# Multi-head attention stage of a four-stage graph kernel: input side one chunk ahead, statistics two ahead, capped rows in two buffers

## The reference

```python
def graph_attention(x, bias, W, a_src, a_dst):
    h = jnp.einsum('bnd,dhk->bhnk', x, W.reshape(D, H, Dh))
    s = jnp.einsum('bhnk,hk->bhn', h, a_src)
    t = jnp.einsum('bhnk,hk->bhn', h, a_dst)
    e = jax.nn.leaky_relu(s[:, :, :, None] + t[:, :, None, :], ALPHA)
    e = e + bias[:, None, :, :]
    attn = jax.nn.softmax(e, axis=-1)
    out = jnp.einsum('bhij,bhjk->bhik', attn, h)
    return out.transpose(0, 2, 1, 3).reshape(B, N, H * Dh)
attn_in = layer_norm(x, g1, b1)
attn = graph_attention(attn_in, bias, W1, a_src1, a_dst1) + x
attn_in2 = layer_norm(attn, g2, b2)
out = graph_attention(attn_in2, bias, W2, a_src2, a_dst2) + attn
```

## Time and profile before

| what | value |
| --- | --- |
| median of 3 runs | 1226.5 us (1225.91 to 1226.75) |
| profiled execution | 1226.1 us, its span 1224.3 us |
| TensorE, VectorE, ScalarE, GpSimd busy | 92%, 64%, 61%, 35% of the span |
| multi-head stage | about 798 to 1078 us of the span |
| single-head stage | about 1078 to the end |

### The profile page before, as it was taken

One profiled execution on the slowest core, in us unless ns is written; L12 is line 12 of the kernel. 1 busy time (PEld: TensorE's weight loads), 2 busy tenths in 40 slices (PEclk: granted clock), 3 DMA queues, 4 the chain that ended last, 5 costly groups with the idle time before them and its releaser, 6 DMA issues.

```text
span 1224.3 us, 41293 instructions
## 1 busy us (share of the span) xinstructions
PE 1127.3 (92%) x16156; PEld 984.7 (80%) x16156; DVE 781.3 (64%) x1908; ACT 743.7 (61%) x1766; POOL 426.7 (35%) x641
## 2 busy tenths in 40 slices
PE   5799999999999899999999999978888888869998
PEld 5588888888888788998998998966667777658886
DVE  6676777777677745545445445456556665558886
ACT  2577767777776645445445446465656656548986
POOL 2532111211121012312212213225566555567664
PEclk9799999999999999999999999998778877779999
DMA  8020100110000000000000000000000000002112
GB/s 224 1 71 29 54 28 28 28 53 28 28 20 12 2 1 1 1 1 0 0 0 0 0 0 0 1 20 21 17 17 9 17 17 10 3 2 70 62 57 86
DMA packets 41736, 31.18 MB, mean 25 GB/s; under 512 B 5280, under 2 KB 41376, under 8 KB 41632
## 3 DMA queue, kind: packets, MB, share of 16 engines
q1 hardware_dynamic: 36736, 28.84, 7.5%
q10 hardware_dynamic: 4896, 0.80, 0.6%
HBM read 21.25 MB, written 8.39 MB: 24 GB/s over the span
## 4 chain that ended last, share of the span: by engine, by line
PE 71%; ACT 9%; DVE 8%; issue 6%; POOL 3%; ACTq 1%; DVEq 1%; DMA 0%; POOLq 0%
PE BK L1320 5%; PE BK L1198 5%; PE BK L1197 5%; PE BK L1196 5%; PE BK L1404 5%; PE BK L1405 5%; PE BK L1406 5%; PE BK L1294 4%; PE F L1196 4%; PE BK L1306 4%; PE F L1221 3%; PE F L1197 3%; PE F L1198 3%; PE BK L1287 3%; ACT xn L1005 2%
## 5 line engine op out<-in xcount | busy, mean ns | idle before, releaser
L862 POOL TENSOR_TENSOR ve<-mv,eps_l 128x4 f32<-128x4 f32 x64 | 15.1, 236 | 533.0 <-DVE mv L300 533.0
L1066 ACT ACTIVATE gf<-BK,bcol 128x512 f32<-128x512 f32 x128 | 88.1, 688 | 178.6 <-PE BK L1198 167.8
L985 ACT ACTIVATE e_sb<-BK,nmx 128x128 f32<-128x128 f32 x512 | 141.4, 402 | 28.5 <-DVE nmx L460 28.5
L1404 PE MATMUL BK<-wf_hi,gh 128*128 128x256 f32 x512 | 142.9, 279 | 0.0
L1405 PE MATMUL BK<-wf_hi,gl 128*128 128x256 f32 x512 | 141.6, 277 | 0.0
L1406 PE MATMUL BK<-wf_lo,gh 128*128 128x256 f32 x512 | 141.5, 276 | 0.0
L553 DVE TENSOR_TENSOR gl<-gf,gh 128x512 fp32r<-128x512 f32 x128 | 93.9, 734 | 64.2 <-ACT gh L1067 62.0
L466 DVE TENSOR_TENSOR pt_sb<-BK,ft 128x512 f32<-128x512 f32 x128 | 85.4, 687 | 66.8 <-PE BK L1294 65.3
L1005 ACT ACTIVATE xn<-x_all,neg_mr,rstd 128x256 f32 (+1 forms) x188 | 99.6, 602 | 24.0 <-POOL neg_mr L871 24.0
L614 DVE SCALAR_TENSOR_TENSOR pp<-BK,gt_all 128x512 f32<-128x512 f32 x128 | 82.5, 678 | 34.3 <-PE BK L1454 31.8
L567 DVE TENSOR_TENSOR x_all<-BK,x_all 128x256 f32 (+1 forms) x64 | 27.2, 425 | 117.0 <-PE BK L1406 117.0
(11 more groups left out here) (211 smaller groups left out, 3060.5 us busy)
## 6 DMA issues: line engine op xcount, KB each, us to landing
x_all<-in_x_dram SPq DMA_DIRECT2D x16, 512.0 KB, 4.4
adj_in<-in_adj_dram SPq DMA_DIRECT2D x32, 256.0 KB, 2.8
out_dram<-y SPq DMA_DIRECT2D x16, 512.0 KB, 2.9
s_wf<-in_L_gnn_Wf_dram SPq DMA_DIRECT2D x2, 1024.0 KB, 11.1
s_w<-in_L_gnn_W_dram SPq DMA_DIRECT2D x2, 256.0 KB, 7.6
s_wq<-in_L_gnn_Wq_dram SPq DMA_DIRECT2D x1, 256.0 KB, 3.6
s_wk<-in_L_gnn_Wk_dram SPq DMA_DIRECT2D x1, 256.0 KB, 4.1
s_wv<-in_L_gnn_Wv_dram SPq DMA_DIRECT2D x1, 256.0 KB, 4.6
```

What stands on the lines that cost most here:

```text
L985: e = act.activation(e_sb[:, j, :], LE[:, r, q, :], ACT.Exp, bias=nmx[:, j:j + 1], scale=1.0)
L1404: pe.matmul(dst, gh[:, f, n], hi[:, f, :], start=(f == 0), stop=False)
```

## The change

The step order of the multi-head stage is written anew on all four engines. The input side of chunk i+1 (transpose, high part, low part) runs at the end of step i, into the second pair of buffers that the single-head stage already has (`xhd`, `xld`). Layer-norm statistics are taken two chunks ahead (`far_stats`); those of chunk 1 stand ahead of the stage, and those of the first chunks of the single-head stage are taken inside the last steps. `row_c` has two buffers. The first pair of inverse rows is made on VectorE, the second stays on ScalarE. The rows are turned between the two halves of the values, into F1. The diff, cut to its core (the step functions `c1_step` in the order VectorE, ScalarE, TensorE; the `elif` branch ahead of ScalarE's is GpSimd's):

```diff
-        row_c = o("row_c", [P, W4])
+        row_c = [o(f"row_c{r}", [P, W4]) for r in range(2)]
...
-            def row_limits(i):
+            def row_limits(i, par):
                 dve.wait_ge(r_e, i + 1)
-                wait_for(dve, r_q, i * 2)
-                dve.tensor_scalar(row_c[:], row_e[:], row_cap[:, 0:1], None, ALU.min).then_inc(r_c, 1)
+                wait_for(dve, r_q, i * 2 - 2)
+                dve.tensor_scalar(row_c[par][:], row_e[:], row_cap[:, 0:1], None, ALU.min).then_inc(r_c, 1)
+            def inverse_rows(i, par):
+                dve.wait_ge(r_c, i + 1)
+                wait_for(dve, r_q, i * 2 - 1)
+                for to, of in ((0, 64), (64, 0)):
+                    r = dve.tensor_scalar(inv[0][to:to + 64, :], row_c[par][of:of + 64, :], half_row[of:of + 64, 0:1], None, ALU.mult)
+                r.then_inc(r_inv[0], 1)
...
+            def far_stats(i):
+                c = i + CC + 2
+                wraps = isinstance(i, int) and i >= NC - 2
+                nxt = i + 2 - NC if wraps else i + 2
+                dve.wait_ge(ln_mv, c * G)
+                if wraps:
+                    dve.wait_ge(c_x, C_START + (nxt + 1) * G)
+                for g in range(G):
+                    stats(c, nxt, g)
+            def lo_part(i, par):
+                for kt in range(KT):
+                    dve.wait_ge(ln_xh, (i + CC) * KT + kt + 1)
+                    dve.tensor_tensor(xld[par][:, kt, :], F[kt][:], xhd[par][:, kt, :].bitcast(F32), ALU.subtract).then_inc(ln_xl, 1)
...
             def c1_step(i, half, par):
+                row_minima(i)
                 if back:
                     c_scale(i - 1, 0)
+                row_shifts(i)
                 if back and not (isinstance(i, int) and i == 1):
                     c_recip(i - 2, par)
                 if back:
-                    c_scale(i - 1, 1)
-                    ln_lo(i + CC)
-                    c_scale(i - 1, 2)
-                    c_scale(i - 1, 3)
-                row_minima(i)
-                next_stats(i, (0, 1))
-                row_shifts(i)
-                next_stats(i, (2, 3))
-                dve.wait_ge(ln_st, (i + CC + 2) * G)
+                    for h in range(1, 4):
+                        c_scale(i - 1, h)
+                row_limits(i, par)
+                inverse_rows(i, par)
+                far_stats(i)
+                dve.wait_ge(ln_st, (i + CC + 3) * G)
+                dve.wait_ge(ln_nm, nm_count(i + CC + 1, CC))
+                dve.wait_ge(c_bq, i + 1)
+                hb_out(i, par, 0)
                 if back:
                     c_scale(i - 1, 4)
-                aggr(i + CC + 1)
-                row_limits(i)
-                if back:
                     c_scale(i - 1, 5)
+                hb_out(i, par, 1)
+                aggr(i + CC + 2)
+                if back:
                     c_scale(i - 1, 6)
                     c_scale(i - 1, 7)
-                dve.wait_ge(c_bq, i + 1)
-                hb_out(i, par, 0)
-                hb_out(i, par, 1)
+                lo_part(i + 1, 1 - par)
...
 +                    elif first == CC:
+                        pool.wait_ge(ln_xn, (i + CC + 2) * G)
+                        rstd_of(i + CC + 2, EPS[CC])
+                        neg_mean_of(i + CC + 2, CC)
...
             def c1_step(i, half, par):
-                if back:
-                    ln_hi(i + CC)
+                normalise(i, CC, range(G))
+                far_minima(i)
                 act.wait_ge(adj_t, i + NC + 1)
                 act.activation(gt_all[:, bass.ds(i * W4, W4)], F[0][:], ACT.Exp).then_inc(c_gt, 1)
+                row_exps(i)
+                bq_out(i, par, 0)
                 if back:
                     c_out_copy(i - 1, 1 - par, 0)
-                far_minima(i)
-                row_exps(i)
-                inverse_rows(i, 0)
-                bq_out(i, par, 0)
+                inverse_rows(i, par)
+                hi_part(i + 1, 1 - par)
                 if back:
                     c_out_copy(i - 1, 1 - par, 1)
-                normalise(i, CC, range(G))
-                inverse_rows(i, 1)
...
             def row_turn(i, par):
                 pe.wait_ge(r_c, i + 1)
-                wait_for(pe, c_pp, i * H - 3)
                 for g in range(G):
-                    r = pe.transpose(BK[:, 0, g * P:(g + 1) * P], row_c[:, g * P:(g + 1) * P], ident[:])
+                    r = pe.transpose(ROW[CC][:, g * P:(g + 1) * P], row_c[par][:, g * P:(g + 1) * P], ident[:])
                 r.then_inc(r_t, 1)
...
             def c1_step(i, half, par):
-                if back:
-                    ratios(i - 1, 0)
-                c_turn(i, CC)
+                c_st(i, CC, 0, par)
+                c_st(i, CC, 1, par)
+                if back:
+                    ratios(i - 1, 1 - par, 0)
+                adj_turn(i + CC, half, par, CC)
                 if back:
                     c_av(i - 1, 1 - par, 0)
-                adj_turn(i + CC, half, par, CC)
-                if back:
                     c_av(i - 1, 1 - par, 1)
-                c_st(i, CC, 0)
-                c_st(i, CC, 1)
+                pe.wait_ge(c_gt, i + 1)
+                c_h_out(0, par)
+                c_h_out(1, par)
+                row_turn(i, par)
                 if back:
                     c_av(i - 1, 1 - par, 2)
                     c_av(i - 1, 1 - par, 3)
-                    ratios(i - 1, 1)
-                pe.wait_ge(c_gt, i + 1)
-                c_h_out(0)
-                c_h_out(1)
+                    ratios(i - 1, 1 - par, 1)
+                pe.wait_ge(c_one, i + 1)
+                c_h_out(2, par)
+                c_h_out(3, par)
                 if back:
                     c_av(i - 1, 1 - par, 4)
-                row_turn(i)
-                pe.wait_ge(r_e, i + 1)
-                c_h_out(2)
-                c_h_out(3)
-                if back:
-                    c_av(i - 1, 1 - par, 5)
-                    c_av(i - 1, 1 - par, 6)
-                    c_av(i - 1, 1 - par, 7)
+                c1_turn(i + 1)
+                if back:
+                    for h in range(5, H):
+                        c_av(i - 1, 1 - par, h)
```

More of the change, by code:

```diff
@@ L599, in hb_out @@
                                   ALU.mult).then_inc(c_hb, 1)
-            def next_stats(i, graphs):
-                final = isinstance(i, int) and i == NC - 1
-                if graphs[0] == 0:
-                    dve.wait_ge(*((c_x, C_START + G) if final else (b_x, (i + 2) * G)))
-                for g in graphs:
-                    stats(i + CC + 1, 0 if final else i + 1, g)
+            def far_stats(i):
[11 more added lines that the diff above has]
+                    dve.tensor_tensor(xld[par][:, kt, :], F[kt][:], xhd[par][:, kt, :].bitcast(F32), ALU.subtract).then_inc(ln_xl, 1)
             def c_scale(i, h):
@@ L655, in _ @@
             dve.wait_ge(c_zero, 6)
+            dve.wait_ge(ln_mv, (CC + 1) * G)
+            for g in range(G):
+                stats(CC + 1, 1, g)
+            dve.wait_ge(ln_st, (CC + 2) * G)
+            aggr(CC + 1)
             chunks(dve, c1_step)
@@ L731, in c2_step @@
                     d_norm(*prev, 3)
-            d_lo(0, 0)
             dve.wait_ge(c_x, C_START + 3 * G)
-            for g in range(G):
-                stats(CD + 1, 1, g)
-            dve.wait_ge(ln_nm, nm_count(CD, CD))
-            dve.wait_ge(ln_st, (CD + 2) * G)
-            aggr(CD + 1)
             dve.wait_ge(ln_mv, (CD + 2) * G)
@@ L893, in norms @@
                             neg_mean_of(i + CD + 2, CD)
+                    elif first == CC:
+                        pool.wait_ge(ln_xn, (i + CC + 2) * G)
+                        rstd_of(i + CC + 2, EPS[CC])
+                        neg_mean_of(i + CC + 2, CC)
                     else:
@@ L927, in residual_sum @@
                         pool.tensor_tensor(xs(i, g), atc[:, g, :], xs(i, g), ALU.add).then_inc(c_x, 1)
+                if first == CC:
+                    pool.wait_ge(ln_xn, (CC + 1) * G)
+                    rstd_of(CC + 1, EPS[CC])
+                    neg_mean_of(CC + 1, CC)
                 chunks(pool, norms)
@@ L1107, in row_exps, with inverse_rows @@
                 r.then_inc(r_e, 1)
-            def inverse_rows(i, t):
+            def inverse_rows(i, par):
                 act.wait_ge(r_c, i + 1)
+                wait_for(act, r_q, i * 2)
                 for to, of in ((0, 64), (64, 0)):
-                    r = act.activation(inv[t][to:to + 64, :], row_c[of:of + 64, :], ACT.Copy, scale=half_row[of:of + 64, t:t + 1])
-                r.then_inc(r_inv, 1)
+                    r = act.activation(inv[1][to:to + 64, :], row_c[par][of:of + 64, :], ACT.Copy, scale=half_row[of:of + 64, 1:2])
+                r.then_inc(r_inv[1], 1)
             def c2_front(i, par):
@@ L1149, in bq_out @@
                 act.wait_ge(*((r_t, i + 1) if layer == 0 else (c_bqt, i + 1)))
```

(28 more changed lines are left out.)

21 lines of the change are left out of this document (10 added, 11 removed).

## The result

The changed kernel takes 1198.3 us, the median of four runs (1196.6 to 1199.9), against 1226.6 us before: a ratio of 0.977 (0.9753 to 0.9787). The forecast was 1192 us, inside a range from 1181 to 1220. The profiled execution took 1198.9 us, its span 1197.0 us, 27.3 us less than before.

What follows compares the result with a forecast made beforehand. It took a serial loop through all engines, 17.07 us a chunk, as the bound. 14 x (14.8 - 17.07) = -31.8, with start +3.0, drain -0.4 and single-head passage -5.0, gave -34.2: 1192 us, range 1181 to 1220.

Steps and rivals of the forecast that it cites:

- The bound and the mechanism: Multi-head stage: one serial loop through all engines sets 17.07 us a chunk; the new order brings it to 14.8.
- The serial stretch of xn: Input side of each multi-head chunk: ScalarE's normalise and the wait on it leave the loop; xn itself takes 2.06 us.
- One sign: Steady multi-head stage: VectorE busy over 75% and waiting mostly for ratios and the high part.
- The loop at full clock, 14.4: Steady multi-head chunk without clock falls: statistics 1.4, ratios 1.4, VectorE's run 8.3, transpose to low parts 3.3 us.
- cap and inverse pair: VectorE in each multi-head chunk: cap set at 0.43 us, moved inverse pair at 0.86, about +0.9 (0.5 to 1.3).
- The clock: TensorE in the multi-head stage: a fall in every second or third chunk, +0.4 us a chunk; mean clock over 0.88.
- The rival in which the clock keeps its share of half: Multi-head stage: TensorE's loop pieces at 1.2 GHz in nearly every chunk, 15.6 to 17.0 us each, 1203 to 1223; chance 0.15.
- Start: First chunks of the multi-head stage: second minimum later, at 818.5 instead of 815.46, +3.0 us (2 to 4).
- Drain: End of the multi-head stage: last chunk's reciprocal 21.8 us behind its minimum instead of 22.2, -0.4 us.
- Passage to the single-head stage: Last reciprocal to second single-head chunk: GpSimd's scale and mean come a step earlier, -5.0 us (0 to -6).
- The GpSimd wait as a rival: ScalarE's normalise waits for GpSimd's mean, each chunk pays 1 us: 15.8 us a chunk, 1206 us; chance 0.07.

Runs made afterwards that it cites:

- e2: Changed kernel with one added GpSimd wait: the residual share starts only when VectorE has written the first inverse rows; 1190.1 us, ratio 0.9698.
- e10: Changed kernel with two 128x512 filler matmuls per step on TensorE, GpSimd's share left where the change has it; 1197.4 us, ratio 0.9744.
- e1: Changed kernel with the first inverse pair back on ScalarE, directly behind row_e, new order kept; 1192.6 us, ratio 0.9717.
- e9: e2 with GpSimd's scale and mean of the second single-head chunk held until VectorE's last multi-head reciprocal; 1194.9 us, ratio 0.9724.
- e5: e2 plus two 128x512 filler matmuls on TensorE ahead of the first head of each chunk; 1186.2 us, ratio 0.9675.

## Why the prediction was right, and where it was off

**The bound and the mechanism: right.** The time fell by 28 us where 34 were forecast. The serial stretch of xn and its wait are gone, VectorE is busy 81% of the steady stage (75% were asked for), the clock is at 0.95 (0.88), and the minimum waits 1.75 us (1.5). One sign was read wrong: VectorE was to wait mostly for ratios and the high part, but it waits 22.8 us for the statistics matmuls, 8.4 for ratios, and the high part is not among its waits. No run puts single parts of the new input side back, so the gain is shown for the order as a whole.

**The loop at full clock, 14.4: right**, 14.38 in e2, though in its parts two errors cancel. By e2's rows: minimum to first scale 1.35 (1.4 forecast), VectorE's run to the end of the values 8.44 (8.3), from there to the statistics matmuls 2.9 (3.3), statistics 1.7 (1.4). The forecast's pace of 0.43 for the cap stands in no row: the earlier trace rows give 0.39 from its start to the next, and in e2 it is 0.60, since the pair waits for the cap's end.

**The term that was mis-sized: cap and inverse pair.** "I take 0.47 with a pace of 0.43 in a queue, so +0.9 us of VectorE per chunk (0.5 to 1.3)". The pair measured 0.98 alone, close enough, and 1.39 beside GpSimd's share, over the upper bound; and the cap, costed at 0.43 from a chunk where GpSimd did something else, took 0.88. The operation's price was read from a row without asking which engine ran beside it, and the new order put GpSimd there. That is 0.81 us in every chunk at full clock. The Trainium skill (SBUF — State Buffer, "Who interferes with whom") says that VectorE and GpSimd share one pair of ports, that `tensor_scalar` can take it in its two-port modes, and that whoever comes second stands still until the other's instruction is done. The traces agree as far as they go: cap and inverses are such instructions, the losses of 0.40 for the cap and 0.2 for each inverse stay under one GpSimd instruction (2.34/4 = 0.59), and the three scales, with an input from PSUM, take 1.8 us with GpSimd beside them too. That it is the port, and no other thing that the two share, no run here tests by itself.

**The clock: right in kind, and its price depends on the rest.** "+0.4" a chunk was forecast. It is 0.39 with the contention gone (14.71 - 14.32), but 0.16 in the changed kernel (15.18 - 15.02), since VectorE's slow pair covers the fall. The rival in which the clock keeps its share of half fell: 0.95. The terms of the steady chunk as the runs give them: 14.32 without either (14.4 in the forecast), + 0.70 for GpSimd with the clock full (15.02 - 14.32, the first chunks without a share in the mean), + 0.16 for the clock = 15.18. The forecast had 14.4 + 0 + 0.4 = 14.8. The difference of 0.38 over 14 chunks is 5.3 us, the steady chunks' miss in the table but for rounding. Some of the forecast's closeness is luck: the term left out (0.70) was partly paid back by a fall that cost 0.24 less than forecast. The prediction also said that the clock is 1.00 in the single-head stage; the earlier trace rows show that from 1105.7 on only, and at the stage's start there were half stretches (below).

**Start: inside its bounds, 0.95 short.** The first minimum is 1.4 us later against the end of stage B, the second 2.5 more. Another 0.9 lies ahead, in the stages that the diff does not touch, and stays unexplained. ScalarE's far minima stand behind xn, and VectorE waits 4.4 us for them:

```profile
808.18 0.22 DVE L586 SCALAR_TENSOR_TENSOR row_sh<-row_mn,own_row,far_mx 128x4 f32<-128x4 f32 x1 [4.41 <-ACT far_mx L1119]
```

**Drain: mis-sized**, +1.45 for -0.4. e2's drain takes 22.15 us, what it took before the change (22.17), so the loss goes with GpSimd's share and the forecast gain never came. The clock does not explain it: e10, with the early share and a granted clock of 0.83 in the drain, takes 23.56, and e2 has 0.84. In e1, with the early share but the pair on ScalarE, it is 22.29, so it is the pair beside the share.

**Passage to the single-head stage: -6.2 for -5.0.** GpSimd's low rows start 10.4 us behind the reciprocal instead of 15.3, which is -4.9 as worked out, but the forecast gave all of it to scale and mean: e9 shows 1.9 for them, and 3.0 stay for VectorE's statistics. Another 1.3 us came behind the low rows, where the statistics matmuls ran at full clock (0.23 us apart) instead of half (0.43).

**The GpSimd wait as a rival** did not come: GpSimd waits for VectorE's aggregation (4.85 us in the chunk shown) and not the other way round. It did harm without one wait, by its mere presence.

## What to carry to other kernels

When an instruction is priced from a row, look at what the neighbouring engines do in that row and what they will do in the new order; VectorE's cap cost 0.48 us alone and 0.87 beside a GpSimd tensor operation, and one wait on GpSimd's side gave the difference back. Remove stalls in the order in which they hide one another: the clock's fall was worth 0.16 us a chunk until the contention was gone, and 0.39 then. When several cures together give less than their sum, read again which waits are left: at 14.2 us a chunk the loop ran for the most part through TensorE, and two different cuts on VectorE ended at the same 14.15.

## What the runs showed of the hardware

- A half-height scaled copy (64x512) took 0.49 us on VectorE, as much as the full-height cap (0.48); half the partitions saved nothing.
- Beside GpSimd's 128x256 operations the cap went from 0.48 to between 0.81 and 0.88, the pair from 0.98 to 1.39 or 1.63, the 128x4 shifts from 0.21 to 0.42; GpSimd's share went from 2.34 to 2.71.
- With two more 128x512 matmuls in each chunk the granted clock was 1.00 through 201 us (e5, e10), in which it had fallen in each second or third chunk without them (0.95 and 0.97).
